# First expert tiles among the attention's last operations, the bias inside the Gelu, and more result batches summed beside the tiles

## The reference

```python
x = x + xattn(layernorm(x), ctx, ctx, W_q..b_o, mask)      # 16 heads, softmax over 77 keys
xn = layernorm(x)
proj = einsum('bsd,ed->bse', xn, Wp)
gate_scores = einsum('bsd,ed->bse', l2norm(proj), l2norm(sim_matrix)) / temperature
top_v, top_i = top_k(gate_scores, 2);  gate_probs = softmax(top_v)
h  = gelu(einsum('bsd,edf->ebsf', xn, W1) + b1)            # 8 experts, 128 -> 512
eo = einsum('ebsf,efd->ebsd', h, W2) + b2                  # 512 -> 128
out = x + sum over the two chosen experts of prob * eo
```

## Time and profile before

| | us |
|---|---|
| three runs | 386.9, 387.59, 391.44 (median 387.59) |
| the profiled execution, its own time | 386.44 |
| its span, first to last instruction | 384.7 |
| PE busy | 341.3 (89%) |
| DVE busy | 304.0 (79%) |
| ACT busy | 291.5 (76%) |
| POOL busy | 276.7 (72%) |

### The profile page before, as it was taken

The page is one execution under the profiler, slowest core; times in us unless marked ns, Lnnn a source line. Parts: engine busy times, 40 slices in busy tenths (PEclk is TensorE's granted clock), DMA queues, the critical chain, the costliest instruction groups (busy, mean ns, idle before and its releaser), DMA issues.

```text
span 384.7 us, 14132 instructions
## 1 busy us (share of the span) xinstructions
PE 341.3 (89%) x3564; PEld 290.9 (76%) x3565; DVE 304.0 (79%) x972; ACT 291.5 (76%) x846; POOL 276.7 (72%) x493
## 2 busy tenths in 40 slices
PE   4799999999999999999997689999999999999800
PEld 3467777777777777777775579999999999999700
DVE  6678999999999999999998647676665666668773
ACT  3799999999999999999986465666566666666621
POOL 5632487777877777777744647888989888789873
PEclk9999999999999999999999869999999999999965
DMA  3132023321333011210000221223222223259156
GB/s 91 44 81 78 23 79 100 100 67 62 97 97 88 33 40 43 85 36 22 23 29 18 64 65 50 65 66 84 73 83 73 69 69 82 56 152 284 33 147 180
DMA packets 42570, 29.19 MB, mean 76 GB/s; under 512 B 5443, under 2 KB 39311, under 8 KB 42528
## 3 DMA queue, kind: packets, MB, share of 16 engines
q1 hardware_dynamic: 34848, 18.60, 18.2%
q0 software_dynamic: 4320, 8.53, 6.6%
q10 hardware_dynamic: 3360, 1.57, 1.4%
HBM read 17.53 MB, written 11.62 MB: 76 GB/s over the span
## 4 chain that ended last, share of the span: by engine, by line
PE 57%; DVE 21%; issue 9%; DMA 4%; ACT 3%; POOL 2%; DVEq 2%; ACTq 0%; SPq 0%; POOLq 0%
PE ps_s L912 15%; PE ps_s L923 13%; PE ps_t L635 7%; PE ps_o L646 4%; PE ps_s L619 4%; DVE sums L1217 3%; DVE mx L1200 3%; PE ps_s L609 3%; DVE rows L1285 2%; PE ps_t L905 2%; PE ps_x L666 1%; DVE pr L1210 1%; DMA ys<-results 1%; PE ps_o L660 1%; DVE x L1239 1%
## 5 line engine op out<-in xcount | busy, mean ns | idle before, releaser
L567 POOL DMA_INDIRECT results<-eo,didx x71 | 70.8, 997 | 22.1 <-POOL didx L556 10.0
L452 POOL DMA_INDIRECT lists<-rows,slots x64 | 66.7, 1043 | 17.7 <-issue 16.9
L912 PE MATMUL ps_s<-xtT,w1c 128*128 128x128 f32 x568 | 78.3, 282 | 1.1 <-DVE xtT L1623 1.0
L923 PE MATMUL ps_s<-w2s,hT 128*128 x568 | 75.8, 277 | 0.2 <-ACT hT L1148 0.2
L963 ACT ACTIVATE pT<-ps_t 77x512 f32<-77x512 f32 x128 | 73.9, 595 | 2.0 <-PE ps_t L635 2.0
L635 PE MATMUL ps_t<-identf,pr 128*77 128x128 f32 x512 | 72.8, 275 | 0.8 <-ACT pT L963 0.7
L912 PEld LDWEIGHTS ps_s<-xtT,w1c 128*128 128x128 f32 x568 | 71.5, 198 | 2.0 <-DVE xtT L1623 1.9
L1144 ACT ACTIVATE w1c<-w1s 128x512 f32 x71 | 44.8, 631 | 35.4 <-PE ps_s L912 34.2
L923 PEld LDWEIGHTS ps_s<-w2s,hT 128*128 128x128 f32 x568 | 69.7, 193 | 0.5 <-issue 0.4
L1637 DVE TENSOR_TENSOR h<-ps_s,b1T 128x512 f32<-128x512 f32 x71 | 49.0, 690 | 25.5 <-PE ps_s L912 23.8
L635 PEld LDWEIGHTS ps_t<-identf,pr 128*77 128x77 f32 x512 | 58.6, 147 | 6.9 <-issue 4.6
(11 more groups left out here) (211 smaller groups left out, 609.3 us busy)
## 6 DMA issues: line engine op xcount, KB each, us to landing
xt<-lists SPq DMA_DIRECT2D x71, 66.0 KB
ys<-results SPq DMA_DIRECT2D x14, 256.0 KB, 3.7
xin<-in_x_dram SPq DMA_DIRECT2D x16, 128.0 KB
w1s<-in_L_ffn_W_dram SPq DMA_DIRECT2D x8, 256.0 KB, 3.2
w2s<-in_L_ffn_W_dram SPq DMA_DIRECT2D x8, 256.0 KB, 3.5
out_dram<-x SPq DMA_DIRECT2D x5, 256.0 KB, 5.6
cin<-in_ctx_dram SPq DMA_DIRECT2D x16, 77.0 KB
results<-eo,didx POOLq DMA_INDIRECT x71
```

Source lines behind the costliest of these rows:

```text
L452: nc.gpsimd.indirect_dma_start(lists, bass.IndirectOffsetOnAxis(ap=slots[:, r, s * TOPK + k:s * TOPK + k + 1], axis=0), rows[:, r, s, k, : ...
L567: nc.gpsimd.indirect_dma_start(results, bass.IndirectOffsetOnAxis(ap=didx[:, r:r + 1], axis=0), eo[:, r, :], None, bounds_check=TOPK * NTO ...
L912: last = nc.tensor.matmul(ps_s[:, r, c * P:(c + 1) * P], w1c[:, r, c * P:(c + 1) * P], xtT[:, r, :], start=True, stop=True)
L923: last = nc.tensor.matmul(ps_s[:, 2 + r, 0:D], hT[:, r, c * P:(c + 1) * P], w2s[:, bass.ds(e + c * D, D)], start=(c == 0), stop=(c == FC - 1))
```

## The change

Three things change. **The bias goes into the Gelu.** DVE's addition into `h` is gone; ACT reads the up product from PSUM in four pieces of 128 columns, each with its own column of b1 as bias, and `w1c` of tile j+2 is copied after the Gelu of tile j. ACT reads the table twice a tile. **The attention's end is written out by hand.** The table is read earlier, and iterations -3 to 1 of the tiles stand among the last pieces of pairs 14 and 15; the places of what is left of pair 15 and of the second table move to later iterations (`between`), and DRAINED goes from 9 to 14. **The tail.** DVE sums 17 batches beside tiles 60 to 70 (one or two a tile), and all of batches 0 to 23; four chunks are stored ahead of the last results; the two last chunks are loaded half by SP and half by ACT; POOL leaves out its last three memsets, and adds only batches 26, 29 and 31.

```diff
-    AHEAD = 3
-    DRAINED = 9
+    DRAINED = 14
     LOOPED = DRAINED + 18
-    EARLY = 11
-    LATER = 3
+    SUMMED = (2, 2, 1, 2, 1, 2, 1, 2, 1, 2, 1)
+    SUMS_FROM = N_TILES - len(SUMMED)
...
         def on_pool(b):
-            return b >= EARLY and b % 8 in POOL_OF_8
+            return b >= PART and b % 8 in POOL_OF_8
...
+        def late_results(eng, k):
+            all_returned(eng, N_TILES)
+            for c in range(PART // CH, NB // CH):
                 eng.dma_start(ys[:, c, k, :, :], res[c, k]).then_inc(y_loaded[c], 16)
...
-            all_returned(sp, N_TILES)
-            load_results(sp, PART // CH)
-            for c in range(LATER, NB // CH):
+            for c in range(sum(SUMMED) // CH):
+                store(sp, c)
+            late_results(sp, 0)
+            for c in range(sum(SUMMED) // CH, NB // CH - 1):
                 store(sp, c)
...
             def between(j):
-                if j == 1:
+                if j in (0, 1, 2, 3):
+                    scatter(NP - 2, NP - 2, j // TOPK, j % TOPK)
+                    nc.gpsimd.memset(pace[:, 2 + j, :], 0.0).then_inc(spaced, 1)
+                    if j == 1:
+                        second_power(NP - 1, NP - 1)
+                elif j == 7:
                     gate_power(NP - 1, NP - 1)
-                elif 8 <= j < 12:
-                    scatter(NP - 1, NP - 1, (j - 8) // TOPK, (j - 8) % TOPK)
+                    destinations(NP - 1, NP - 1)
+                elif j in (14, 16, 18, 20):
+                    k = (j - 14) // 2
+                    scatter(NP - 1, NP - 1, k // TOPK, k % TOPK)
+                    pool.wait_ge(spaced, 4)
+                    nc.gpsimd.memset(pace[:, 2 + k, :], 0.0).then_inc(spaced, 1)
```

In PE's `tile(j, m)`:

```diff
                     after_tile(pe, FE["w1c_ready"], j + 1)
-                    after_tile(pe, FE["h_ready"], j - 1)
+                    after_tile(pe, FE["act_ready"], j - 1)
```

ACT's `tile`:

```diff
+            def tile(j, m):
+                r = m % 2
+                if has(j, 0, N_TILES):
+                    e = act.value_load(tab_w[0:1, j:j + 1] if known(j) else tab_w[0:1, bass.ds(j, 1)],
+                                       min_val=0, max_val=(NE - 1) * F)
+                    after_tile(act, FE["up_done"], j)
+                    after_tile(act, FE["down_done"], j - 2)
+                    settled(act)
+                    for c in range(FC):
+                        last = nc.scalar.activation(hT[:, r, c * P:(c + 1) * P], ps_s[:, r, c * P:(c + 1) * P], ACT.Gelu,
+                                                    bias=b1T[:, bass.ds(e // P + c, 1)])
+                    last.then_inc(FE["act_ready"], 1)
+                if has(j, 2, N_TILES):
+                    b = j + 2
+                    e = act.value_load(tab_w[0:1, b:b + 1] if known(b) else tab_w[0:1, bass.ds(b, 1)],
+                                       min_val=0, max_val=(NE - 1) * F)
+                    after_tile(act, FE["up_done"], j)
+                    settled(act)
+                    nc.scalar.activation(w1c[:, r, :], w1s[:, bass.ds(e, F)], ACT.Copy).then_inc(FE["w1c_ready"], 1)
```

In DVE's `tile(j, m)` and `between(j)`:

```diff
-                    nc.vector.tensor_tensor(h[:, r, :].rearrange("p (c t) -> p c t", c=FC),
-                                            ps_s[:, r, :].rearrange("p (c t) -> p c t", c=FC),
-                                            b1T[:, bass.ds(e1, FC)].unsqueeze(2).to_broadcast([P, FC, P]), ALU.add
-                                            ).then_inc(FE["h_ready"], 1)
+                if known(j) and SUMS_FROM <= j < N_TILES:
+                    sum_batches(sum(SUMMED[:j - SUMS_FROM]), sum(SUMMED[:j - SUMS_FROM + 1]))
...
-                if j == -1:
+                if j == 3:
                     second_norm(NP - 1, NP - 1)
-                elif j == 3:
+                elif j == 8:
                     gates(NP - 1, NP - 1)
                     best(NP - 1)
```

436 lines of the change are left out of this document (286 added, 150 removed).

## The result

The changed kernel takes **402.43 us** (median of four runs, 401.22 to 403.04) where the kernel before took 389.51 beside it; the ratio is 1.033 [1.025, 1.042]. A second group of runs gave 402.13 against 390.57, 1.031 [1.026, 1.036]. Forecast were 390, with 398 as the upper end: the change is slower by more than I allowed. The profiled execution took 401.22, its span is 399.4.

The account below looks back on a forecast made before the run. PE bounds the tiles before; after the change a circle of waits gives 2.03 us a tile. Last down product 369.6 plus tail 18.3 is a span of 387.9, plus 1.7 is 389.6, say 390 us; range 381 to 398.

Parts of the forecast that it names:

- The first tiles: Handover: table made about 6 us earlier, first up product about 212, tile 3's at 222.5, 7.0 earlier than before.
- The wait at the gates: Ahead of tile 11: DVE waits some 5.6 us for POOL's gate_power, leaving all but 0.3 us of the handover's gain gone.
- no fall of the clock: PE keeps full clock in handover and gates' wait; the rival, a fall there, had 394.6 us and chance 0.24.
- one of my own signs of a wrong forecast: Whole kernel: forecast wrong if tiles keep 1.90, gates finds rn ready, or the clock falls anywhere.
- The circle: Tiles: down product, Gelu, copy, up product and down product wait in turn; 4.09 us for two tiles, 2.03 taken each.
- One of my signs: Tiles from 260 us on: PE under 96% busy, up products 2.0 us or more apart, waiting for w1c.
- The reads run ahead: ACT's table reads start while earlier instructions are queued, so its sequencer needs 1.83 us a tile, under 1.90.
- the second rival: ACT's loop: reads don't run ahead, a tile takes 2.24, 11.6 us more for 55 tiles, 401 us; chance 0.12.
- The tail: From last down product to span's end: 20.8 us becomes 18.3, by 1.9 less lag of POOL and 0.6 off the rest.
- The start: Profiled execution of the kernel before: span 384.7, execution 386.44, 1.15 under the median 387.59, left within the range.
- the circle's upper bound (2.24): Tiles: the most a tile takes, 0.67 + 0.76 + 3 x 0.25 + 0.05, if reads don't run ahead on ACT.

Follow-up runs that it names:

- the second execution: The changed kernel, unchanged, profiled again; from the attention's last values product to the end it took 202.1 us.
- the run with gates later: Changed kernel with the last pair's gates, and all that follows from them, three tiles later; 397.58 us, ratio 1.019 to the kernel before.
- the copy first: Changed kernel with ACT's w1c copy for tile j+2 ahead of the Gelus of tile j; 396.1 us, ratio 1.014 to the kernel before.
- four hT: Changed kernel with four hT buffers instead of two, Gelus waiting for the down product of tile j-4; 396.57 us, ratio 1.017 to the kernel before.
- the bias alone: Kernel before with the bias in four Gelus and no h on DVE: copy ahead of them 390.07 us (1.002), behind them 399.13 us (1.022).
- the same kernel: Changed kernel, gates later, bias on DVE up to tile 60, in the Gelus from 61; 396.74 us (0.983), again 391.44 us (1.004), to the kernel before.

## Why the prediction was wrong

To compare, 3.0 us are taken off the times of the profiled execution, whose values product was at 199.5 and not 196.5.

- **The first tiles.** Forecast 212, 222.5 and 224.5 for the first up product, that of tile 3 and the first eo; it was 211.9, 222.4 and 224.8. The trace confirms the handover's order. I had counted no fall of the clock there, and there was one (214.4 to 217.8). In the second execution it wasn't there, and the up product of tile 3 came 25.5 us behind the values instead of 25.9; so the fall cost some 0.4 us, and that the times meet so closely is partly luck.
- **The wait at the gates.** Forecast 5.6 us for DVE, 4.1 for PE and tile 11 at 245.7; it was 5.07, 3.49 and 247.05. The mechanism held, POOL was 1.2 us later than my sum, and the run with gates later showed its worth. What I took from it, no fall of the clock, was right for this execution and wrong for two others, where the fall cost 2.6 us. The falls at 214.4 and 234.9 stood in no term either; the second cost 1.5 us at tile 6. That the clock falls anywhere was one of my own signs of a wrong forecast.
- **The circle.** Right in its path, as the runs with the copy first, with four hT and with the bias alone show. **The step that failed is its sum, 4.09 us for two tiles or 2.03 a tile, which has no term for the loop.** Where the tiles are written out it came true: tiles 14 to 25 took 2.03 each. In the loop they took 2.14 on the mean from 31 to 60. The rows above are from the loop: 1.11 from the first Gelu to the copy (1.1 forecast), 0.63, 0.22 to PE (0.13), and 2.21 from the up product at 303.79 to the next Gelu but one at 306.00 (1.87 and 0.36, so 2.23), 4.17 in all. ACT's timeline where the tiles are written out:

```profile
260.33 1.14 ACT L1168 ACTIVATE hT<-ps_s,b1T 128x128 f32<-128x128 f32 x4 [0.37 <-issue]
261.37 0.63 ACT L1177 ACTIVATE w1c<-w1s 128x512 f32 x1
```

Here the copy starts 1.04 behind the first Gelu; in the loop ACT has one register instruction more ahead of the table read, and the same step is 1.11 or 1.12. The down product takes 1.15 in the loop by its rows and 1.06 here. The rest of the 2.14 lies in single tiles of 2.2 to 2.4, as where ACT's loop turns (tile 41 came 2.14 and tile 42 2.39 behind the one before). Writing tiles 32 to 51 out gave back 0.09 a tile. From tile 15 to 70 the miss is 4.8 us, the largest part. One of my signs didn't come: PE under 96% busy. It was 99.50, by ends that are modelled.
- **The reads run ahead.** They do: in the changed kernel the second rival's 2.24 a tile did not come. ACT's trace shows it: the read for the copy starts while the Gelus of its tile are still running. That its 401 is near the measured time is chance. (Its 2.24 should have read 2.23 by its own terms.) From the figures of the Trainium skill, "ScalarE: Activation LUTs", What ACT_TABLE_LOAD costs, I had an estimate of 0.29 from Gelu to Gelu; in the trace they start 0.25 apart, as I took them, and the 2.07 a tile worked out from it is near the truth for another reason.
- **The tail.** Forecast 18.3, measured 399.4 less 379.6 = 19.8. The first load of results came 4.6 us behind the last product, not 3: the table read of the last eo stood behind the sums (0.85 of idle with "issue" in front of it), and POOL's last write began at 381.86. Timelines of DVE, POOL and SP:

```profile
380.76 0.29 DVE L1632 TENSOR_TENSOR eo<-ps_s,b2s 128x128 f32<-128x128 f32 x1 [0.85 <-issue]
```

```profile
381.86 1.08 POOL L580 DMA_INDIRECT results<-eo,didx  x1 [0.80 <-issue]
```

```profile
384.22 0.92 SPq L277 DMA_DIRECT2D ys<-results  x2
```

- **The start.** I built on one execution whose attention was the earliest of the classes; 3.0 us of the difference between 389.6 and 401.22 are that (the clock was at 0.50 from 13.0 to 23.2, see the last section), and I had put only 1.15 into the range for it.

Together: 3.0 start, 1.3 up to tile 11, 0.3 to tile 15, 4.8 rate, 0.6 behind tile 70, 1.5 tail, 11.5 of 11.6. No single term leaves the range: with the rate's 4.8 the forecast would have been 394.4, with the start 397.4, and the gates and the tail put it above 398. But the rate and the start alone use up nearly all of the room, and the range held neither: the circle's upper bound (2.24) was given to a rival with 0.12, and of the start only 1.15 was in it.

## What to carry to other kernels

When an instruction that waits for a late result is put ahead of one that releases the next product, follow the circle of waits around two buffers; reorder the two, or add buffers, before anything else: here one exchange was worth 9 us of 390. A sum of latencies on such a circle is a lower bound: in a loop each engine adds register work that the written-out part doesn't have. It cost 0.09 to 0.11 us a tile here with the circle closed, and as much with it open, where ACT was the second bound; the kernel before, bound by PE alone, kept 1.90 in its loop. Count stages from a common event, and compare versions only within one group of runs: the same kernel gave 0.983 in one and 1.004 in another.
